# Lookups, gram parts and dense layers in another order on TensorE: a DLRM tower on one core

## What is computed

```
e = jnp.stack([tbl_f[ids[:, f]] for f in 0..31], axis=1)      # [2048, 32, 256]
dots = einsum('bnd,bmd->bnm', e, e)[:, iu, ju]                  # 496 pairs, i < j
h = concatenate([dots, dense_ctx], axis=1)                      # [2048, 512]
h = maximum(h @ W_top1 + b_top1, 0)                             # 512 -> 512
h = maximum(h @ W_top2 + b_top2, 0)                             # 512 -> 256
y = h @ W_top3                                                  # 256 -> 1
```

## Time and profile before

| | |
|---|---|
| median of 3 runs | 896.95 us (895.36 to 898.39) |
| the profiled execution | 892.55 us, its span 890.7 us |
| PE busy | 601.0 us (67% of the span) |
| PE weight loads | 524.1 us (59%) |
| DVE, ACT, POOL busy | 225.9, 204.6, 398.0 us |
| mean granted TensorE clock | 0.850 of full speed |

### The profile page before, as it was taken

How to read it: one execution, slowest core, us unless ns; L and a number is a source line. 1 busy time by engine, 2 the same in 40 slices (tenths; PEclk the granted TensorE clock), 3 DMA queues, 4 the chain that set the end, 5 groups by cost and what they waited for, 6 DMA issues and landing times.

```text
span 890.7 us, 24184 instructions
## 1 busy us (share of the span) xinstructions
PE 601.0 (67%) x11019; PEld 524.1 (59%) x11019; DVE 225.9 (25%) x578; ACT 204.6 (23%) x369; POOL 398.0 (45%) x426
## 2 busy tenths in 40 slices
PE   3557668486684867748577584875848668486687
PEld 2456557375572756737467474765737657375586
DVE  3444313123130231402223032231312313123122
ACT  4252303103030030401313022130210303103042
POOL 7563625526255361543715347262462625526220
PEclk9688969698796987969789697896969969698799
DMA  9962312313122141321313224131231312313110
GB/s 220 243 204 68 99 42 77 94 44 102 43 78 83 50 107 38 83 73 56 108 37 87 63 57 118 32 96 49 70 105 39 101 41 76 88 41 90 43 38 2
DMA packets 37459, 70.97 MB, mean 80 GB/s; under 512 B 10382, under 2 KB 23438, under 8 KB 37358
## 3 DMA queue, kind: packets, MB, share of 16 engines
q0 software_dynamic: 20112, 54.95, 22.1%
q1 hardware_dynamic: 17246, 14.48, 7.0%
HBM read 69.39 MB, written 0.01 MB: 78 GB/s over the span
## 4 chain that ended last, share of the span: by engine, by line
PE 42%; another core or an unknown queue 30%; issue 13%; ACT 12%; DMA 1%; DVE 1%; POOL 1%; ACTq 0%; DVEq 0%
PE look_ps L338 18%; PE quad_ps L358 12%; PE top_ps L420 6%; ACT turned L501 4%; ACT turned L483 3%; PE turn_ps L322 3%; PE quad_ps L322 2%; ACT area L550 2%; ACT ahead L490 1%; DMA rows<-in_tbl,row_ids 1%; PE quad_ps L377 1%; POOL rows L295 1%; PE top_ps L407 1%; ACT products L506 0%
## 5 line engine op out<-in xcount | busy, mean ns | idle before, releaser
L295 POOL DMA_INDIRECT rows<-in_tbl,row_ids x419 | 397.2, 948 | 458.1 <-PE turn_ps L322 184.1
L338 PE MATMUL look_ps<-one_hot,small 125*128 125x256 f32 (+1 forms) x1536 | 251.9, 303 | 104.7 <-issue 92.8
L338 PEld LDWEIGHTS look_ps<-one_hot,small 125*128 125x128 f32 x1536 | 214.0, 202 | 116.6 <-issue 112.3
L358 PE MATMUL quad_ps<-turned 128*32 128x31 f32 x7680 | 140.0, 204 | 121.8 <-issue 121.5
L358 PEld LDWEIGHTS quad_ps<-turned 128*32 128x32 f32 x7680 | 108.8, 115 | 166.9 <-issue 153.3
L674 DVE TENSOR_SCALAR one_hot<-ids_across,sub_row 125x256 fp32r<-125x256 int32 (+1 forms) x384 | 112.0, 364 | 145.8 <-PE look_ps L338 126.6
L322 PE MATMUL turn_ps<-ident,rows 128*128 128x128 f32 x424 | 64.5, 282 | 28.5 <-issue 14.7
L655 DVE TENSOR_TENSOR top_ps<-top_ps,b_sb 128x256 f32<-128x256 f32 x15 | 6.5, 433 | 299.8 <-PE top_ps L420 299.8
L490 ACT ACTIVATE ahead<-look_ps 128x512 f32<-128x512 f32 (+1 forms) x48 | 28.3, 590 | 232.5 <-PE look_ps L338 219.1
L407 PE MATMUL top_ps<-area,w_sb 128*128 128x128 f32 x488 | 61.9, 276 | 19.5 <-issue 18.8
L550 ACT ACTIVATE area<-top_ps,b_sb 128x128 f32<-128x128 f32 x61 | 17.5, 368 | 227.5 <-remote 225.2
(11 more groups left out here) (50 smaller groups left out, 169.9 us busy)
## 6 DMA issues: line engine op xcount, KB each, us to landing
rows<-in_tbl,row_ids POOLq DMA_INDIRECT x419
ids_across<-in_small_ids SPq DMA_DIRECT2D x45, 128.0 KB
landed<-in_tbl SPq DMA_DIRECT2D x6, 896.0 KB
w_sb<-in_W_top SPq DMA_DIRECT2D x4, 256.0 KB
landed<-in_tbl SPq DMA_DIRECT2D x6, 104.0 KB
w_sb<-in_W_top SPq DMA_DIRECT2D x1, 512.0 KB
area<-in_dense_ctx SPq DMA_DIRECT2D x16, 8.0 KB
row_ids<-in_ids SPq DMA_DIRECT2D x1, 240.0 KB
```

Source lines behind the costliest of these rows:

```text
L295: pool.indirect_dma_start(out=rows[:, n % PLACES, j, :], out_offset=None, in_=tables[f], in_offset=bass.IndirectOffsetOnAxis(ap=row_ids[:, ...
L338: last = pe.matmul(look_ps[:, c * width:(c + 1) * width], small[:, f, r, part, c * P:(c + 1) * P], one_hot[n % 2][:, r, 0:width], start=(r ...
L358: last = pe.matmul(gram_ps[q * FIELDS:(q + 1) * FIELDS, g // BANK_GROUPS, at:at + COLS], turned[:, c, s, :], turned[:, c, s, 0:COLS], star ...
```

## The change

For tiles 1 to 14, TensorE's work between the unit turns is put in another order:

- Each of the tile's three lookups stands whole (32 products) ahead of gram parts 0, 1 and 2 (in tile 0 its two ahead of parts 0 and 1).
- `layer1(t - 1)` leaves `turn_all`; its quarters stand behind gram parts 3, 4, 5 and 6.
- `layer2(t - 1)` stands behind part 7 instead of part 0.
- ScalarE copies the first two lookups before `keep_hidden1`, and VectorE makes all three one-hot sets before `last_layers`.

The last tile keeps its order. Nothing is added or removed.

```diff
+    LAYER1_BEHIND = 3
+    LAYER2_BEHIND = 7
...
-                for m in range(M1):
-                    layer1(t - 1, m)
+                if t == TILES - 1:
+                    for m in range(M1):
+                        layer1(t - 1, m)
 
             def look_between(t, k):
 
-                made = FIRST[t + 1] - FIRST[t]
-                for n in range(made):
-                    begin, end = (n * (PARTS + 1) + made - 1) // made, ((n + 1) * (PARTS + 1) + made - 1) // made
-                    if begin <= k < end:
-                        look_up(FIRST[t] + n, PRODUCTS * (k - begin) // (end - begin),
-                                PRODUCTS * (k + 1 - begin) // (end - begin))
+                if k < FIRST[t + 1] - FIRST[t]:
+                    look_up(FIRST[t] + k, 0, PRODUCTS)
...
-                    if t > 0 and k == 0:
+                    if 0 < t < TILES - 1 and LAYER1_BEHIND <= k < LAYER1_BEHIND + M1:
+                        layer1(t - 1, k - LAYER1_BEHIND)
+                    if t > 0 and k == (0 if t == TILES - 1 else LAYER2_BEHIND):
                         layer2(t - 1)
...
-                look_between(t, PARTS)
...
-                    keep_hidden1(t - 1)
+                    if t == TILES - 1:
+                        keep_hidden1(t - 1)
+
+                act.wait_ge(placed, 2 * t + 1)
                 for n in range(FIRST[t], FIRST[t + 1] - 1):
                     keep_looked_up(n)
+                if 0 < t < TILES - 1:
+                    keep_hidden1(t - 1)
...
-                    if k == 0 and t > 0:
-                        last_layers(t - 1)
-                if t == TILES - 1:
+                if t > 0:
                     last_layers(t - 1)
```

## The result

| | before | changed |
|---|---|---|
| median | 896.15 us (894.34 to 898.39, 4 runs) | 1033.85 us (1021.18 to 1035.69, 4 runs) |
| ratio | | 1.1505 (1.1409 to 1.1601) |
| profiled execution, its span | 892.55, 890.7 us | 1033.76, 1032.0 us |
| mean granted TensorE clock | 0.850 | 0.765 |

The forecast was 926 us. The sign was right, the size was not: 137 us were lost where the sum had 29.

The account below looks back on a forecast made before the run. Gathers holding PE were taken to bound the 54.6 us tile. Terms 0 + 0 + 1.9 + 0.2 + 0 = 2.1 us a tile, 29 us in 14 tiles, gave 926 us; own range 905 to 950, full range 872 to 962.

Parts of the forecast that it names:

- Gathers hold PE: In each tile's long run of 18 gathers PE goes slow, 17.70 us in the tile cut; early units' gathers leave holes.
- Faster by much: Rival: the slow stretch belongs to layer 1 with the lookup behind it and goes; about 700 us, chance 0.07.
- Point 1: In the slow stretch a lookup takes layer 1's place at much the same cost: 0, between -0.4 and +0.3 us.
- Point 2: Layer 2 moves to full clock, 1.99 us instead of 3.40, but a lookup fills the low clock: no gain.
- Point 3: At the tile's end unfolding waits for layer 2 and the last layer, delaying the features: 1.9 us a tile.
- Point 4: Whole lookups share one bank; a gram part nearly covers ScalarE's copy between two of them: +0.2 us.
- Point 5: Holes behind the four early units, 1.3 us each, stay as they were: 0, bounds -5.2 and +4 us a tile.
- The upper bound of +4 us: Cost a tile if the early units' eight gathers close up to a run and PE goes slow in it.
- The eight gathers close up: Rival: the early units' gathers form a second slow stretch in each tile; 6.1 us a tile, 982 us, chance 0.10.
- The faster rival that the holes go: Layer 1's long records carry PE over the holes behind early units: 854 us, with half 890; chance 0.14.

Follow-up runs that it names:

- the second experiment: The changed kernel with its lookups left in nine pieces as before, so only layers 1 and 2 are moved: 943.16 us, ratio 1.0541 against the kernel before.

## Why the prediction was wrong, point by point

- **Gathers hold PE** (what bounds the kernel now): right on the chips of the result. Plain transfers of the same bytes take the slow stretch and the holes away. It is not a property of the kernel alone, which the profile of one chip could not tell. "Faster by much", the rival that the slow stretch is layer 1's, is out by the same runs.
- **Point 1, layer 1 against a lookup, 0:** right; the stretch from the first gather to the slow stretch's end is 25.5 us against 25.3. It ends 3.3 us behind the 18th gather. It holds because a whole lookup took layer 1's place; with a piece in its place the second experiment lost 3.4 us a tile.
- **Point 2, no gain from layer 2:** mis-sized. The term set layer 2 at full clock (1.99 us) against a lookup drawn out by the low clock. The lookup is drawn out (5.61 us against 4.07), but layer 2 is not at full clock either: the low clock came again behind the uncovered gram parts, and it takes 3.43 us. That is 1.4 us in the tile shown, where the term had 0.
- **Point 3, 1.9 us a tile:** the mechanism was right and the size too high, 27 us in all. The features' wait grew by 14.7 us, taking the step away gave about 16 us back, and where nothing holds PE the wait grew by 19.2 and 20.4 us. Unfolding starts 4.3 us behind gram's end instead of 2.8, which is layer 2 at low clock. The features follow it after 2.3 us (361.10 to 363.44) instead of 3.2, since ScalarE, which had copies to make before its pick until 314.28, now begins it at once (362.35). The forecast's step from "2.8 us behind the gram's end" to 5.1 us for the features needs this, and doesn't say it.
- **Point 4, +0.2 us:** not seen by itself; no wait for ScalarE's copy of a lookup is among the changed kernel's longer ones.
- **Point 5, "I take the holes to stay: 0":** this step failed. I took the 1.3 us that stood idle in the earlier trace rows for the price of two gathers. It was the remainder after the lookup piece had covered the rest; the price is about 2.5 us, and three to four holes stand behind each early unit where I named two. Four parts take 1.1 us more each (3.2 against 2.1), 4.4 us a tile or 61 us in 14. The upper bound of +4 us was set for another mechanism and without the clock: with the holes PE fell to 1.2 GHz for a second stretch of 13 us, and PE's busy time grew by 80.6 us, some 20 of them inside these parts. In the tile shown the three units and two quarters of layer 1 in that stretch take some 3.1 us more than at full clock. Rows of that kind stood in the trace already: the earlier trace rows shows the clock at 0.64 in the one stretch with long holes. I had written that the gathers, being the same eight, cost the same, and left out that what a hold costs is set by what stands in it.
- **The rivals:** none came. "The eight gathers close up" gave 982 by a longer run of gathers; the gathers stayed in pairs with idle time of POOL between (3.1 to 3.9 us), so its mechanism is out though its time was the nearest. The faster rival that the holes go was wrong for the reason just given: layer 1's quarter stands behind the light records, not ahead of them.
- **Slips that change nothing:** "without a hole" for the 8.5 us from the first unit to layer 1's end overlooks the 0.42 us of the earlier trace rows, and 0.4 us a tile gives a lower end of 903, not 905.
- On a free chip the forecast's +29 us lies near the 22 measured, and that is in part luck: the wait that it priced at 27 us grew by 19.2, and shorter waits for gathered rows, which no term had, took 12.9 us off. With plain transfers the same order lost 35 us.

## What to carry to other kernels

A hole in a row of light instructions is what a hold costs after the cover ahead of it; before moving heavy work away from an event that stalls the engine, price the stall with nothing in front of it, and ask whether the extra holes bring the clock down. Where gathers hold TensorE, put heavy products directly behind what triggers a gather, and light ones far from it; where they don't, the same order only pays for its own waits. Don't take a sum of waits by instruction for a cause: idle time moves to whatever stands in its place. And time an order on more than one chip: here the kernel before ran in 896 or 563 us, and one reordering gave -5% on one kind and +5% on the other.

## What the runs showed of the hardware that I had not expected

- While two indirect gathers were at work, TensorE took up six light records in some 0.75 us and stood 0.4 to 0.5 us of it, on two chips besides the result's runs, and not with plain transfers: 896 us with the gathers against 535 with the same 20112 packets as plain transfers from the same engine.
- On three other chips the same gathers, each of the same 0.95 us, made no slow stretch, and the kernel took 563 us (a kernel in its order, 567.3 us of span, had a clock of 0.982). What differs between the chips isn't known from these runs, nor whether the index form or the scattered rows do it.
- Holes of 0.3 to 0.5 us in the gram part at full clock (335.60 to 339.33) were followed by 13 us at a granted clock of 0.50; the gram parts of before, with two such holes each, ran at 1.00 (350.81 to 368.15).
